# Expert blocks numbered in the order in which they fill, and scatter and store in turn on GpSimd

## The chip, the cores and the metric

The kernel runs on one core of a Trainium2 chip. Its time is the device time of one launch in microseconds; three runs of the kernel before gave 1337.54 (median), 1336.7 and 1342.43. Durations below are from one profiled execution of it, which took 1341.81 us, with a span of 1339.8 us in the trace.

## The reference

4096 tokens of width 128 (16 sequences of 256) go through four residual layers: a linear attention with an MLP, a mixture of 8 experts, a self-attention with relative positions, and the same mixture of experts again. The change is about the two expert layers:

```
logits = t @ switch_w + switch_b              # t: 4096 x 128, normalised
routes = argmax(softmax(logits));  p = max(softmax(logits))
for e in range(8):
    h = gelu(t @ w1[e] + b1[e])               # 128 -> 512
    y = h @ w2[e] + b2[e]                     # 512 -> 128
    out = where(routes == e, y, out)
x = x + out * p
```

Each token needs only the expert it is routed to.

## The kernel before, in words

Tokens lie in SBUF as `rows`, 32 tiles of 128 tokens (one token per partition), a row of 258 words each: the normalised token, the residual x, the token's number (as a count from the end) and its probability. An expert layer has two stages, each a block of engine programs; a stage begins when every engine has ended the stage before.

`route_tokens` (VectorE mostly) finds each token's expert, counts the tokens of each expert per tile, takes running sums over tiles (L249), and gives each token a slot. All slots of an expert lie together, and each expert starts at a multiple of 128, so that 40 blocks of 128 slots are enough for any route. A table `bexp` has the expert of each block (L269 to L272).

`run_experts` moves and computes. GpSimd scatters the 32 tiles with indirect DMAs into `slots_in`, an array of 40x128 rows in HBM that was cleared before (L326), and afterwards stores the 40 results (L321), each when y of its block is ready. SyncE first loads and stores the position tables of the next layer (`early`, in the first expert layer alone), waits for all 32 scatters, and then loads the 40 blocks (L340) into four buffers in turn; load k waits for y of block k-4. VectorE reads the block's expert number into a register (L418) and copies that expert's 1156 weights per partition into one of four buffers (L420), copies the transposed block out of PSUM (L426), and makes y from the second product (L432 to L435). TensorE transposes (L358) and does four products up (L366) and four down (L374); ScalarE does the gelu (L405). The order on each engine is written out by hand in `step`: block k's products up, block k+1's transpose, block k-1's products down on TensorE; expert k+2, transposed copy k+1, result k-1 on VectorE. Four blocks are unrolled, the first and last four outside a loop.

In the second expert layer the same code runs without the position tables, and the stores go to the kernel's output. Names begin with 0f or 1f for the layer, and fr and fe for the two stages.

Of the kernel before, what the change touches and what calls it, by code (L numbers as in the profile page):

```python
# [34 lines left out]
X_AT, LEFT_AT, PROB_AT = D, 2 * D, 2 * D + 1  # L35
ROW = 2 * D + 2
# [133 lines left out]

def route_tokens(nc, prefix, norm, con, L, sbias, w, WA, s_weights, prob, slot, bexp):

    with ExitStack() as stack:
# [10 lines left out]
        nblk_i = m.sb("nblocks_i", [P, E], I32)  # L184
        pre = [m.sb(f"blockprefix{i}", [P, 4 + E]) for i in range(2)]
        pos = m.sb("pos", [P, TILES, E])
        offs = m.sb("offs", [P, E])
        slotf = m.sb("slotf", [P, TILES])
        ge = m.sb("ge", [P, BLOCKS, E])
        bexpf = m.sb("bexpf", [P, BLOCKS])  # L190
# [23 lines left out]
        def _(dve):  # L214
# [26 lines left out]
            dve.memset(pre[0][:, 0:4], 0.0)  # L241
            then(dve.memset(pre[1][:, 0:4], 0.0))
# [9 lines left out]
            then(dve.tensor_scalar(nblk_i[:, :], tot[:, PAD + TILES - 1, :], float(P - 1), None, ALU.add))  # L252
            then(dve.tensor_scalar(nblk_i[:, :], nblk_i[:, :], 7, None, ALU.arith_shift_right))
            then(dve.tensor_copy(pre[0][:, 4:], nblk_i[:, :]))
            for k in range(3):
                a, b = pre[k % 2], pre[(k + 1) % 2]
                then(dve.tensor_tensor(b[:, 4:], a[:, 4:], a[:, 4 - (1 << k):4 + E - (1 << k)], ALU.add))
            bend = pre[1]

            then(dve.tensor_scalar(offs[:, :], bend[:, 3:3 + E], float(P), None, ALU.mult))  # L260
            then(dve.tensor_tensor(pos[:, :, :], tot[:, PAD:, :], cfirst[:, :, :], ALU.subtract))
            then(dve.tensor_tensor(pos[:, :, :], psr, pos[:, :, :], ALU.add))
            then(dve.tensor_tensor(pos[:, :, :], pos[:, :, :], offs[:, :].unsqueeze(1).to_broadcast(TE), ALU.add))
            then(dve.tensor_tensor(pos[:, :, :], pos[:, :, :], hot[:, :, :], ALU.mult))
            then(dve.tensor_reduce(slotf[:, :], pos[:, :, :], AX.X, ALU.add))
# [9 lines left out]
def run_experts(nc, prefix, rows, norm, con, WA, s_weights, slot, bexp, slots_in, tokens, s_cleared, again, tables=None):  # L275
# [3 lines left out]
    with ExitStack() as stack:  # L279
# [38 lines left out]
        def _(pool):  # L318
# [13 lines left out]
        def _(sp):  # L332
# [10 lines left out]
            if early:  # L343
                early.stored(sp)
# [1276 lines left out]
```

## Time and profile before

| | |
|---|---|
| median of 3 runs | 1337.54 us |
| profiled execution, its time / span | 1341.81 / 1339.8 us |
| busy share: TensorE, VectorE, ScalarE, GpSimd | 79%, 70%, 51%, 42% |
| DMA | 165.92 MB, mean 124 GB/s |
| scatters and block loop of the first expert layer | 182.8 to 328 us |
| the same of the second | 1187.9 to 1332 us |

Between the two lies the self-attention, which the change leaves alone but for a few semaphores. A time in the trace is the start of an instruction, counted from the start of the span. The busy time of a DMA instruction on GpSimd (DMA_INDIRECT) is the time in which it writes the transfer's descriptors; the data land later. "idle ... <-X" in a row is what the engine waited for last; "issue" means that it waited for nothing which the profile shows.

### The profile page before, as it was taken

What the parts mean: (1) busy time and instruction counts of PE and PEld (TensorE: products, weight loads), DVE (VectorE), ACT (ScalarE), POOL (GpSimd) and SP (SyncE); (2) the same over time, 40 slices, a digit from 0 to 9 for tenths busy, and PEclk for the clock granted to TensorE, in tenths of its full rate; (3) what the DMA queues carried; (4) which work ended last, traced back from release to release, by engine and by line L of the source; (5) the groups of instructions that cost most, each with busy time, mean ns of one, the idle gap of its engine ahead of it and who ended that gap; (6) DMA issues with size and microseconds to landing.
All of it is one profiled execution on the core that took longest, in us unless ns stands there. A gap on an engine that the chain in (4) does not pass through costs nothing. (4 is left out here: it accounts for less than half of the span.)

```text
span 1339.8 us, 31386 instructions
## 1 busy us (share of the span) xinstructions
PE 1055.2 (79%) x9281; PEld 887.9 (66%) x9281; DVE 938.7 (70%) x2968; ACT 683.0 (51%) x1705; POOL 567.5 (42%) x502
## 2 busy tenths in 40 slices
PE   3993621886444999999999999999999997801986
PEld 2892501886323788888878888888888885701886
DVE  6786641665662888888888888888888887430664
ACT  2346310444271666666666666666666664110443
POOL 2503145454000645455545545455555542045544
PEclk9997555999585999999999999999999999555999
DMA  5910053222178475665656575755656540052221
GB/s 138 231 40 1 1 209 118 73 82 77 46 300 199 114 176 137 157 156 140 161 138 168 132 177 134 162 148 145 165 137 170 128 103 1 0 193 91 79 76 52
DMA packets 75275, 165.92 MB, mean 124 GB/s; under 512 B 8250, under 2 KB 54785, under 8 KB 66529
## 3 DMA queue, kind: packets, MB, share of 16 engines
q1 hardware_dynamic: 69600, 152.75, 44.3%
q0 software_dynamic: 5632, 12.67, 2.8%
q8 instruction: 19, 0.31, 0.1%
q14 instruction: 24, 0.19, 0.0%
HBM read 130.76 MB, written 35.67 MB: 124 GB/s over the span
## 5 line engine op out<-in xcount | busy, mean ns | idle before, releaser
L1150 POOL TENSOR_SCALAR ds_scores<-ds_scores,ds_max 128x256 f32<-128x256 f32 x256 | 348.6, 1362 | 327.0 <-DVE ds_max L1369 326.8
L1361 DVE TENSOR_TENSOR ds_p2c<-ds_bank,ds_p2c 128x512 f32<-128x512 f32 x256 | 175.2, 684 | 80.2 <-PE ds_bank L1199 79.5
L1369 DVE CUSTOM_DVE_ANT_0 ds_scores<-ds_bank,ds_p2c 128x256 f32<-128x256 f32 x512 | 195.8, 419 | 0.2 <-DVE ds_p2c L1361 0.2
L1310 ACT ACTIVATE all_xt<-ds_bank 128x512 f32<-128x512 f32 x256 | 154.2, 602 | 76.3 <-PE ds_bank L1217 72.5
L1199 PE MATMUL ds_bank<-all_constants,ds_c2p_t 128*128 128x128 f32 x1024 | 159.0, 278 | 0.0
L1217 PE MATMUL ds_bank<-all_constants,ds_scores 128*128 128x128 f32 x1024 | 154.1, 272 | 1.8 <-ACT all_xt L1310 1.6
L1199 PEld LDWEIGHTS ds_bank<-all_constants,ds_c2p_t 128*128 128x128 f32 x1024 | 116.2, 141 | 35.8 <-issue 24.3
L1217 PEld LDWEIGHTS ds_bank<-all_constants,ds_scores 128*128 128x128 f32 x1024 | 119.5, 140 | 6.8 <-issue 2.2
L1190 PE MATMUL ds_bank<-ds_qr,ds_tab 64*128 64x128 f32 x1024 | 76.2, 289 | 34.2 <-DVE ds_qr L1345 30.0
L1292 ACT ACTIVATE ds_c2p_t<-ds_bank 128x256 f32<-128x256 f32 x256 | 77.8, 398 | 46.6 <-PE ds_bank L1190 46.6
L1206 PE MATMUL ds_bank<-ds_ks,ds_qs 72*128 72x256 bf16 x512 | 98.3, 273 | 1.1 <-DVE ds_max L1369 1.1
L1376 DVE TENSOR_SCALAR ds_scores<-ds_scores,ds_max 128x256 f32<-128x256 f32 x256 | 97.4, 380 | 0.0
L1190 PEld LDWEIGHTS ds_bank<-ds_qr,ds_tab 64*128 64x128 f32 x1024 | 63.9, 191 | 47.9 <-issue 39.6
L405 ACT ACTIVATE 1fe_h<-1fe_bank,1fe_expert 128x128 f32<-128x128 f32 x160 | 45.7, 369 | 96.0 <-PE 1fe_bank L366 96.0
L1292 ACT ACTIVATE ds_p2c<-ds_bank 128x256 f32<-128x256 f32 x256 | 77.6, 389 | 31.3 <-PE ds_bank L1190 31.3
L405 ACT ACTIVATE 0fe_h<-0fe_bank,0fe_expert 128x128 f32<-128x128 f32 x160 | 45.7, 369 | 87.9 <-PE 0fe_bank L366 87.9
L1345 DVE TENSOR_TENSOR ds_qr<-ds_qr,all_constants 128x2048 f32<-128x2048 f32 x32 | 73.2, 2287 | 19.7 <-DMA ds_qr<-scratch_qk 19.7
L1190 PE MATMUL ds_bank<-ds_kr,ds_tab 64*128 64x128 f32 x1024 | 74.9, 286 | 2.3 <-ACT ds_p2c L1292 1.4
L1345 DVE TENSOR_TENSOR ds_kr<-ds_kr,all_constants 128x2048 f32<-128x2048 f32 x32 | 73.2, 2287 | 4.6 <-DMA ds_kr<-scratch_qk 4.6
L321 POOL DMA_INDIRECT tokens<-0fe_y,0fe_token x40 | 50.2, 1255 | 55.2 <-DVE 0fe_y L435 47.8
L321 POOL DMA_INDIRECT out<-1fe_y,1fe_token x40 | 49.4, 1234 | 55.7 <-DVE 1fe_y L435 47.8
L1190 PEld LDWEIGHTS ds_bank<-ds_kr,ds_tab 64*128 64x128 f32 x1024 | 62.6, 188 | 13.1 <-issue 13.1
(253 smaller groups left out, 2149.0 us busy)
## 6 DMA issues: line engine op xcount, KB each, us to landing
ds_qr<-scratch_qk SPq DMA_DIRECT2D x32, 1024.0 KB, 10.7
ds_kr<-scratch_qk SPq DMA_DIRECT2D x32, 1024.0 KB, 13.7
ds_tab<-scratch_tables SPq DMA_DIRECT2D x64, 248.0 KB, 9.6
slots_in<-all_zero SPq DMA_DIRECT2D x2, 5160.0 KB, 37.7
ds_qs<-scratch_q_parts SPq DMA_DIRECT2D x32, 288.0 KB
ds_ks<-scratch_k_parts SPq DMA_DIRECT2D x32, 288.0 KB
0fe_xb<-slots_in SPq DMA_DIRECT2D x40, 129.0 KB
1fe_xb<-slots_in SPq DMA_DIRECT2D x40, 129.0 KB
```

The costliest lines, as they stand in the source:

```text
L321: pool.indirect_dma_start(tokens, bass.IndirectOffsetOnAxis(ap=token[i][:, 0:1], axis=0), y[i][:, :], None, bounds_check=TOKENS - 1, oob_i ...
L1150: pool.tensor_scalar(S[b % NS][:, 1, :], S[b % NS][:, 1, :], mx[:, 2 * b + 1:2 * b + 2], None, ALU.subtract).then_inc(s_sub1, 1)
L1190: last = pe.matmul(pb[tile][:, :].rearrange("p (r a n) -> p r a n", r=2, a=4)[:, :, a, :], TAB[half][rows, kind, c:c + P], own, start=True ...
L1199: last = pe.transpose(pt1[b % 2][:, st * SEQ + kt * P:st * SEQ + (kt + 1) * P], CT[half][:, kt, b, st * P:(st + 1) * P], con["ident"])
L1206: last = pe.matmul(pqk[b % 2][:, st * SEQ:(st + 1) * SEQ], QS[half][:, b * SEQ + st * P:b * SEQ + (st + 1) * P], KS[half][:, b * SEQ:(b + ...
L1217: last = pe.transpose(pt2[:, kt * SEQ + st * P:kt * SEQ + (st + 1) * P], S[b % NS][:, st, kt * P:(kt + 1) * P], con["ident"])
L1292: last = act.activation(dst, pb[tile][:, at * 64:(at + count) * 64].rearrange("p (g b s) -> p g b s", g=count, b=HALF), ACT.Copy)
L1310: act.activation(PT[b], pt2[:, :].rearrange("p (k s) -> p k s", k=2), ACT.Exp).then_inc(s_exp, 1)
L1345: dve.tensor_tensor(rows, rows, con["own_pos"].unsqueeze(1).to_broadcast([P, HT // 16, 16]), ALU.mult).then_inc(s_masked, 1)
L1361: dve.tensor_tensor(z, pt1[b % 2][:, :].rearrange("p (a k) -> p a k", a=2), z, ALU.add).then_inc(s_z, 1)
L1369: last = dve.tensor_tensor_reduce(out=S[b % NS][:, st, :], in0=pqk[b % 2][:, st * SEQ:(st + 1) * SEQ], in1=PC[half][:, st, b, :], scale=1. ...
L1376: dve.tensor_scalar(S[b % NS][:, 0, :], S[b % NS][:, 0, :], mx[:, 2 * b:2 * b + 1], None, ALU.subtract).then_inc(s_sub0, 1)
```

## The change

Blocks get their numbers in the order in which tiles fill them. After each tile, every expert whose count passes a multiple of 128 has filled a block, and the blocks filled by a tile are numbered by expert; blocks that stay open at the end come last. The number of blocks that can be complete after t tiles has a lower bound for any route, so block k holds only tokens of the first k+8 tiles. Four things follow in the code:

- VectorE's routing has more steps: from the running sums it makes, per tile and expert, how many blocks are full, what number the block now open will get (the next block filled, by a running minimum from behind), and from that each token's slot. The table of experts by block goes; the expert's number is a 259th word of each row, and VectorE reads it from the loaded block.
- SyncE's load of block k waits for the landing of tile k+7's scatter and of the three before, by four semaphores in turn, instead of all 32.
- GpSimd issues 12 scatters, then one scatter and one store in turn until scatter 31, then the remaining stores. A scatter waits until the one four before has landed.
- VectorE's `step` has transposed copy k+1, result k-1, expert k+2, and the last waits for the data of block k+2.

FIRST_TILES is 8; `rising` is 6, so the loads of groups 0 to 5 (blocks 0 to 23) wait tile by tile and the others for all. The parts of the routing that are left out are three prefix steps over the experts (of `open` and `fresh`), and operations of the same size as those shown. Beside it, the add-and-normalise stage uses one semaphore instead of several, and SyncE's wait for the position tables' stores at the first expert layer's end is gone.

```diff
+FIRST_TILES = E
...
             tot = cnt[1]
-            then(dve.tensor_scalar(nblk_i[:, :], tot[:, PAD + TILES - 1, :], float(P - 1), None, ALU.add))
-            then(dve.tensor_scalar(nblk_i[:, :], nblk_i[:, :], 7, None, ALU.arith_shift_right))
-            then(dve.tensor_copy(pre[0][:, 4:], nblk_i[:, :]))
...
+            then(dve.tensor_copy(full_i[:, :, :], tot[:, PAD:, :]))
+            then(dve.tensor_scalar(full_i[:, :, :], full_i[:, :, :], 7, None, ALU.arith_shift_right))
+            then(dve.tensor_copy(full[:, 1:, :], full_i[:, :, :]))
+            dve.tensor_reduce(total[:, :], full[:, :, :], AX.X, ALU.add)
+            dve.scalar_tensor_tensor(before[:, :, :], full[:, 0:TILES, :], -float(P), tot[:, PAD - 1:PAD + TILES - 1, :], ALU.mult, ALU.add)
...
+            then(dve.tensor_tensor(fresh[0][:, :, 4:], full[:, 1:, :], full[:, 0:TILES, :], ALU.subtract))
...
+            for i in range(2):
+                last = dve.tensor_tensor(number[i][:, TILES:, :], ...)
+            then(dve.tensor_tensor(number[0][:, 0:TILES, :], fresh[1][:, :, 3:3 + E], total[:, 0:TILES].unsqueeze(2).to_broadcast(TE), ALU.add))
+            then(dve.tensor_tensor(over[:, :, :], full[:, 1:, :], full[:, 0:TILES, :], ALU.subtract))
...
+            for k in range(5):
+                a, b = number[k % 2], number[(k + 1) % 2]
+                then(dve.tensor_tensor(b[:, 0:TILES, :], a[:, 0:TILES, :], a[:, 1 << k:TILES + (1 << k), :], ALU.min))
+            then(dve.tensor_tensor(place[:, :, :], psr, before[:, :, :], ALU.add))
...
-            then(dve.tensor_tensor(ge[:, :, :], con["iota_b"]..., bend[:, 4:]..., ALU.is_ge))
-            then(dve.tensor_reduce(bexpf[:, :], ge[:, :, :], AX.X, ALU.add))
-            then(dve.tensor_scalar(bexp[:, :], bexpf[:, :], float(E - 1), None, ALU.min))
...
+            def scatter(t):
+                if t >= UNROLL:
+                    pool.wait_ge(s_scat[t % UNROLL], 16 * (t // UNROLL))
+                pool.indirect_dma_start(slots_in, bass.IndirectOffsetOnAxis(ap=slot[:, t:t + 1], axis=0),
+                                        rows[:, t, :], None).then_inc(s_scat[t % UNROLL], 16)
             pool.wait_ge(s_cleared, 16)
-            for t in range(TILES):
-                pool.indirect_dma_start(...).then_inc(s_scat, 16)
+            ahead = FIRST_TILES + UNROLL
+            for t in range(ahead):
+                scatter(t)
             for k in range(BLOCKS):
+                if ahead + k < TILES:
+                    scatter(ahead + k)
                 store(k // UNROLL, k % UNROLL)
...
-            sp.wait_ge(s_scat, 16 * TILES)
...
+            def load_behind(g, i):
+                for t in range(i + FIRST_TILES - UNROLL, i + FIRST_TILES):
+                    sp.wait_ge(s_scat[t % UNROLL], 16 * (g + t // UNROLL + 1))
+                sp.sem_inc(s_go_sp, 1)
+                load(g, i)
+            rising = (TILES - FIRST_TILES) // UNROLL
...
             def expert(g, i):
-                e = dve.value_load(bexp[0:1, bass.ds(UNROLL * g + i, 1)], min_val=0, max_val=E - 1)
+                dve.wait_ge(s_x[i], 16 * (g + 1))
+                dve.sem_inc(s_go_dve, 1)
+                e = dve.value_load(xb[i][0:1, EXPERT_AT:EXPERT_AT + 1].bitcast(I32), min_val=0, max_val=E - 1)
...
-                if i < UNROLL - 2 or more:
-                    expert(g + (i + 2) // UNROLL, (i + 2) % UNROLL)
                 if i < UNROLL - 1 or more:
                     transposed(g + (i + 1) // UNROLL, (i + 1) % UNROLL)
                 if i > 0:
                     result(g, i - 1)
                 elif not isinstance(g, int) or g > 0:
                     result(g - 1, UNROLL - 1)
+                if i < UNROLL - 2 or more:
+                    expert(g + (i + 2) // UNROLL, (i + 2) % UNROLL)
```

How the instructions stand in a row shows it at three places. GpSimd in the first expert layer, before (slots_in0 is the array of slots, tokens the array of results; the number behind a name is the buffer):

```order
L326 DMA slots_in0<-all_rows,0f_slot 5120x258 [waits all_cleared0]
L326 DMA slots_in0<-all_rows,0f_slot 5120x258 x31
L321 DMA tokens<-0fe_y_0,0fe_token_0 4096x128 [waits fe_y]
L321 DMA tokens<-0fe_y_1,0fe_token_1 4096x128 [waits fe_y]
L321 DMA tokens<-0fe_y_2,0fe_token_2 4096x128 [waits fe_y]
```

and now:

```order
L353 DMA slots_in0<-all_rows,0f_slot 5120x259 [waits 0fe_scattered3]
L353 DMA slots_in0<-all_rows,0f_slot 5120x259 [waits 0fe_scattered0]
L347 DMA tokens<-0fe_y_0,0fe_token_0 4096x128 [waits fe_y]
L353 DMA slots_in0<-all_rows,0f_slot 5120x259 [waits 0fe_scattered1]
L347 DMA tokens<-0fe_y_1,0fe_token_1 4096x128 [waits fe_y]
L353 DMA slots_in0<-all_rows,0f_slot 5120x259 [waits 0fe_scattered2]
L347 DMA tokens<-0fe_y_2,0fe_token_2 4096x128 [waits fe_y]
L353 DMA slots_in0<-all_rows,0f_slot 5120x259 [waits 0fe_scattered3]
```

All 32 scatters stood ahead of the first store; now 13 do, and from there each store has a scatter behind it.

SyncE in the same layer, before (xb is the buffer of a loaded block; scratch_far_f belongs to the position tables):

```order
L941 DMA scratch_far_f<-dt_far_parts 16x8x256 x3
L340 DMA 0fe_xb_0<-slots_in0 128x258 [waits 0fe_scattered]
L340 DMA 0fe_xb_1<-slots_in0 128x258
L306 ISA
L340 ISA [waits fe_y]
L340 DMA 0fe_xb_0<-slots_in0 128x258
L315 REGISTER_ALU
L340 ISA [waits fe_y]
```

and now:

```order
L987 DMA scratch_far_f<-dt_far_parts 16x8x256 x3
L373 DMA 0fe_xb_0<-slots_in0 128x259 [waits 0fe_scattered3,0fe_scattered2,0fe_scattered0,0fe_scattered1]
L373 DMA 0fe_xb_1<-slots_in0 128x259 [waits 0fe_scattered0,0fe_scattered3,0fe_scattered1,0fe_scattered2]
L385 ISA
L341 ISA [waits 0fe_scattered3,0fe_scattered2,0fe_scattered0,0fe_scattered1]
L373 ISA [waits fe_y]
L373 DMA 0fe_xb_0<-slots_in0 128x259
L341 REGISTER_ALU [waits 0fe_scattered0]
L373 ISA [waits fe_y]
L373 DMA 0fe_xb_1<-slots_in0 128x259
```

The wait for one counter of all scatters has become four waits ahead of each load; the position tables' stores stand ahead of the first load as before.

VectorE at the first results of the first expert layer, before (expert_ is the weights' buffer, xbt the transposed block):

```order
L426 COPY 0fe_xbt_0<-0fe_bank0 128x128 [waits fe_h,fe_xt]
L432 TENSOR_TENSOR 0fe_y_0<-0fe_bank4,0fe_expert_0 128x128 [waits fe_yp]
L433 TENSOR_SCALAR 0fe_token_0<-0fe_xb_0 128x1
L435 SCALAR_TENSOR_TENSOR 0fe_y_0<-0fe_y_0,0fe_xb_0 128x128 [waits fe_yb]
L418 TENSOR_LOAD 0f_block_expert
L418 ISA x2
L420 ISA [waits fe_y]
L420 COPY 0fe_expert_0<-0f_weights 128x1156
L426 COPY 0fe_xbt_1<-0fe_bank1 128x128 [waits fe_h,fe_xt]
```

and now:

```order
L476 COPY 0fe_xbt_0<-0fe_bank0 128x128 [waits fe_h,fe_xt]
L482 TENSOR_TENSOR 0fe_y_0<-0fe_bank4,0fe_expert_0 128x128 [waits fe_yp]
L483 TENSOR_SCALAR 0fe_token_0<-0fe_xb_0 128x1
L485 SCALAR_TENSOR_TENSOR 0fe_y_0<-0fe_y_0,0fe_xb_0 128x128 [waits fe_yb]
L468 TENSOR_LOAD 0fe_xb_3 [waits fe_x3]
L468 ISA x2
L470 ISA
L470 COPY 0fe_expert_3<-0f_weights 128x1156
L476 COPY 0fe_xbt_1<-0fe_bank1 128x128 [waits fe_h,fe_xt]
```

The register load came from the table and waited for nothing, and its copy for y; it now comes from the block's own data and waits for their landing (fe_x3), one block nearer to their use.

## Rows read from the trace of the kernel before

**Rows 1.** Windows: busy us by engine (instructions), clock granted, DMA share, GB/s.
```profile
182.80:226.00 43.20, 5.26 (x9) 2.06 (x9) 8.25 (x21) 1.96 (x3) 31.87 (x32) 0.50 0.39 132
1187.90:1230.20 42.30, 0.00 (x0) 0.00 (x0) 1.52 (x2) 0.54 (x1) 31.29 (x32) 0.50 0.28 100
1230.20:1331.50 101.30, 87.62 (x680) 81.07 (x680) 62.91 (x198) 45.74 (x160) 47.51 (x39) 0.96 0.27 73
```

**Rows 2.** Instructions on slots_in: ns min/median/max, first and last start.
```profile
L340 SPq DMA_DIRECT2D 1fe_xb<-slots_in x40: 328/333/432, 1230.2 to 1324.1; - x40
L326 POOL DMA_INDIRECT slots_in<-all_rows,0f_slot x32: 956/961/1562, 182.8 to 223.2; - x32
L326 POOL DMA_INDIRECT slots_in<-all_rows,1f_slot x32: 957/961/1364, 1187.9 to 1227.7; - x32
```

**Rows 3.** Timeline: start, us, engine, line, instruction [idle before <-releaser].
```profile
182.81 1.14 POOL L326 DMA_INDIRECT slots_in<-all_rows,0f_slot  x1 [37.21 <-POOLq L173]
...
223.17 0.96 POOL L326 DMA_INDIRECT slots_in<-all_rows,0f_slot  x1 [0.30 <-issue]
226.05 17.81 SPq L340 DMA_DIRECT2D 0fe_xb<-slots_in  x8
...
228.03 0.47 PE L358 MATMUL 0fe_bank<-all_constants,0fe_xb 128*128 128x128 f32 x1 [29.12 <-DMA 0fe_xb<-slots_in]
...
236.04 0.35 DVE L435 SCALAR_TENSOR_TENSOR 0fe_y<-0fe_y,0fe_xb 128x128 f32<-128x128 f32 x1
...
327.06 0.35 DVE L435 SCALAR_TENSOR_TENSOR 0fe_y<-0fe_y,0fe_xb 128x128 f32<-128x128 f32 x1
...
1240.02 0.35 DVE L435 SCALAR_TENSOR_TENSOR 1fe_y<-1fe_y,1fe_xb 128x128 f32<-128x128 f32 x1
...
1331.14 0.35 DVE L435 SCALAR_TENSOR_TENSOR 1fe_y<-1fe_y,1fe_xb 128x128 f32<-128x128 f32 x1
```

**Rows 4.** Timeline of layer 0 at the end of the position tables.
```profile
203.50 1.53 DVE L420 COPY 0fe_expert<-0f_weights 128x1156 f32 x2 [0.32 <-issue]
203.59 1.90 SPq L941 DMA_DIRECT2D scratch_far_f<-dt_far_parts  x3
```

**Rows 5.** Line L418 in 262.2 to 263.2, then VectorE's timeline.
```profile
L418 DVEq TENSOR_LOAD <-0f_block_expert x1: 402/402/402, 262.4 to 262.4; - x1
...
261.14 0.76 DVE L420 COPY 0fe_expert<-0f_weights 128x1156 f32 x1 [0.88 <-DVE 0fe_y L435]
...
262.33 0.35 DVE L435 SCALAR_TENSOR_TENSOR 0fe_y<-0fe_y,0fe_xb 128x128 f32<-128x128 f32 x1
...
263.28 0.76 DVE L420 COPY 0fe_expert<-0f_weights 128x1156 f32 x1 [0.59 <-DVE 0fe_y L435]
```

**Rows 6.** Timeline of VectorE in layer 0's routing.
```profile
169.34 0.29 DVE L230 TENSOR_SCALAR 0fr_cand<-all_logits 128x256 f32<-128x256 f32 x1
...
174.03 2.26 DVE L249 TENSOR_TENSOR 0fr_count<-0fr_count 128x256 f32<-128x256 f32 x5
...
181.31 0.18 DVE L272 TENSOR_SCALAR 0f_block_expert<-0fr_bexpf 128x40 int32<-128x40 f32 x1
```

**Rows 7.** GpSimd's stores: their group in 240 to 320, then timeline.
```profile
L321 POOL DMA_INDIRECT tokens<-0fe_y,0fe_token x34 | 43.9, 1290 | 38.2 <-DVE 0fe_y L435 31.8 <-issue 6.4
...
261.03 0.99 POOL L321 DMA_INDIRECT tokens<-0fe_y,0fe_token  x1 [1.20 <-DVE 0fe_y L435]
263.45 1.43 POOL L321 DMA_INDIRECT tokens<-0fe_y,0fe_token  x1 [1.43 <-DVE 0fe_y L435]
...
290.05 1.03 POOL L321 DMA_INDIRECT tokens<-0fe_y,0fe_token  x1 [1.20 <-DVE 0fe_y L435]
...
328.57 0.97 POOL L321 DMA_INDIRECT tokens<-0fe_y,0fe_token  x1 [0.30 <-issue]
```

**Rows 8.** Windows around the end of the linear attention.
```profile
110.00:114.00 4.00, 1.93 (x14) 1.52 (x12) 2.54 (x9) 0.97 (x2) 0.00 (x0) 1.00 0.00 0
114.00:118.00 4.00, 0.00 (x0) 0.00 (x0) 1.43 (x7) 3.11 (x8) 0.89 (x2) 0.77 0.01 2
```

More of the change, by code:

```diff
@@ L183, in route_tokens @@
         cfirst = m.sb("counts", [P, TILES, E])
[L184 to L187, printed above, removed]
+        before = m.sb("before", [P, TILES, E])
+        full_i = m.sb("full_i", [P, TILES, E], I32)
+        full = m.sb("full", [P, 1 + TILES, E])
+        total = m.sb("total", [P, 1 + TILES])
+        fresh = [m.sb(f"fresh{i}", [P, TILES, 4 + E]) for i in range(2)]
+        open_ = [m.sb(f"open{i}", [P, 4 + E]) for i in range(2)]
+        number = [m.sb(f"number{i}", [P, TILES + PAD, E]) for i in range(2)]
+        place = m.sb("place", [P, TILES, E])
+        over = m.sb("over", [P, TILES, E])
         slotf = m.sb("slotf", [P, TILES])
-        ge = m.sb("ge", [P, BLOCKS, E])
-        bexpf = m.sb("bexpf", [P, BLOCKS])
         bank = m.banks(2)
@@ L260, in _ @@
[L260 to L265, printed above, removed]
@@ new lines, in _ @@
+            then(dve.tensor_tensor(fresh[0][:, :, 4:], full[:, 1:, :], full[:, 0:TILES, :], ALU.subtract))
+            then(dve.tensor_scalar(open_[0][:, 4:], open_[0][:, 4:], 0.0, None, ALU.is_gt))
+            for k in range(3):
+                for a, b, whole in ((open_[k % 2], open_[(k + 1) % 2], (slice(None),)), (fresh[k % 2], fresh[(k + 1) % 2], (slice(None), slice(None)))):
+                    last = dve.tensor_tensor(b[(*whole, slice(4, None))], a[(*whole, slice(4, None))],
+                                             a[(*whole, slice(4 - (1 << k), 4 + E - (1 << k)))], ALU.add)
+                then(last)
@@ new lines, in _ @@
+            none = number[0][:, TILES:TILES + 1, :].to_broadcast(TE)
+            then(dve.tensor_tensor(number[0][:, 0:TILES, :], number[0][:, 0:TILES, :], none, ALU.subtract))
+            then(dve.tensor_tensor(number[0][:, 0:TILES, :], number[0][:, 0:TILES, :], over[:, :, :], ALU.mult))
+            then(dve.tensor_tensor(number[0][:, 0:TILES, :], number[0][:, 0:TILES, :], none, ALU.add))
+            for k in range(5):
+                a, b = number[k % 2], number[(k + 1) % 2]
+                then(dve.tensor_tensor(b[:, 0:TILES, :], a[:, 0:TILES, :], a[:, 1 << k:TILES + (1 << k), :], ALU.min))
@@ new lines, in _ @@
+            then(dve.tensor_tensor(place[:, :, :], psr, before[:, :, :], ALU.add))
+            dve.tensor_scalar(over[:, :, :], place[:, :, :], float(P), None, ALU.is_ge)
+            then(dve.tensor_tensor(before[:, :, :], number[1][:, 1:1 + TILES, :], number[1][:, 0:TILES, :], ALU.subtract))
+            then(dve.scalar_tensor_tensor(over[:, :, :], before[:, :, :], 1.0, over[:, :, :], ALU.subtract, ALU.mult))
+            then(dve.tensor_tensor(over[:, :, :], over[:, :, :], number[1][:, 0:TILES, :], ALU.add))
@@ L279, in run_experts @@
+            then(dve.scalar_tensor_tensor(place[:, :, :], over[:, :, :], float(P), place[:, :, :], ALU.mult, ALU.add))
+            then(dve.tensor_tensor(place[:, :, :], place[:, :, :], hot[:, :, :], ALU.mult))
+            then(dve.tensor_reduce(slotf[:, :], place[:, :, :], AX.X, ALU.add))
+            then(dve.tensor_copy(slot[:, :], slotf[:, :]))
+def run_experts(nc, prefix, rows, norm, con, WA, s_weights, slot, slots_in, tokens, s_cleared, again, tables=None):
     with ExitStack() as stack:
@@ L701, in add_normalised @@
         shift = m.sb("shift", [P, 2 * TILES])
-        s_diff, s_sq, s_var, s_sum, s_ve, s_std, s_rstd, s_neg, s_shift, s_norm, s_gain, s_x = (m.sem(n) for n in (
-            "diff", "square", "var", "sum", "vareps", "std", "rstd", "neg", "shift", "norm", "gain", "x"))
+        s_v, s_ve, s_std, s_shift, s_norm, s_gain, s_x = (m.sem(n) for n in (
+            "v", "vareps", "std", "shift", "norm", "gain", "x"))
         GT = norm.GT
```

77 lines of the change are left out of this document (38 added, 39 removed).

## The prediction

> **What bounds the kernel now.** I read four views. First the page's span, then the windows of the two expert stages: each begins with some 43 us in which GpSimd scatters 32 tiles of rows and TensorE hardly works (5.26 us of 43.20, and 0.00 of 42.30), and only then come 101 us of block loop [rows 1]. Next the instructions on slots_in: 32 scatters at a median of 0.961 us, and in layer 1 the first load at 1230.2, behind the last scatter at 1227.7 [rows 2]. The timeline around that seam gives the latencies: the last scatter starts at 223.17 and lasts 0.96, the first load starts at 226.05 (landing and wake: 1.92), its transpose at 228.03 (1.98 from load to data), and y of block 0 (L435) ends at 236.39, in layer 1 at 1240.37 [rows 3]. So the loop waits for all scatters, by one wait on SyncE. In the loop TensorE is busy 87.62 us for 40 blocks, 2.19 each [rows 1], and y comes about every 2.4 us, so TensorE and the round of VectorE around it set the pace. GpSimd is used 47.51 us of 101.3 there [rows 1]: it follows.
>
> **The change, part by part.** Three terms: the loop starts earlier, the routing before it gets longer, and in the first half of the loop GpSimd has two DMAs to issue per block.
>
> *Earlier start.* A load of block k now waits for tiles up to k+7. Counted from the first scatter, which starts at 182.81 and 1187.9 [rows 2, 3]: the eighth starts 9.04 later (the first pitch is 1.14 and 0.30, six are 0.96 and 0.30 and a little), ends 0.96 later and is seen 1.92 later: 11.9. In layer 1 this is the start of the first load, where before it was 42.3. In layer 0 SyncE first has the position tables to store: its last three issues start at 203.59 and take 1.90 [rows 4], so the load starts at 205.6, which is 22.8 instead of 43.2. The expert number is now read from the loaded block, so VectorE's first two weight copies, which stood finished in the wait before (203.50, layer 0 [rows 4]), fall behind the landing: two copies of 0.76 and, ahead of the first, a register load. From its start to its copy's I estimate 0.7: it lasts 0.40 itself, and the one at 262.4 had its copy at 263.28, 0.9 later, with a wait for y in between [rows 5]. I take 1.7 us in layer 0 (all four loads leave at once) and 2.2 in layer 1 (the second load is 1.27 behind the first). With y of block 0 10.3 and 10.2 us after the load before [rows 3], it now comes at 22.8+10.3+1.7 = 34.8 and 11.9+10.2+2.2 = 24.3, against 53.6 and 52.5 before.
>
> *Longer routing.* Behind the running sums (L249), VectorE ran to the end of L272: 176.3 to 181.5, 5.2 us [rows 6]. In its place stand about 27 operations on 256 elements and some small ones. From L249, five of them in 2.26, one with its wait costs 0.46; a copy or scalar operation 0.33 (0.29 of L230 and the wait); a scalar_tensor_tensor, by 0.35 for 128 elements [rows 3] and 0.13 more, 0.53. Three casts and shifts 1.1; sum, base, open and fresh 1.6; three prefix steps of a small and a large one 1.7; fill, number, over and three combinations 2.8; five minima 2.3; place to slot 3.8: 13.3. That is **8.1 us more in each layer**, on the path, since GpSimd starts behind the stage's end. The five more short fills lie in VectorE's wait for the counts' matmul; uncovered they cost about 0.5 by their sizes.
>
> *GpSimd in the loop.* Scatters 12 to 31 now alternate with stores 0 to 18, and tile k+7, the last that load k needs, stands behind store k-6 and the y it waits for. GpSimd's pair costs at least 0.96+0.30 and 0.97+0.30 (the store at 328.57 came with its y long ready: idle 0.30 [rows 7]), 2.53. The stores of the loop take 1.29 on average, not 0.97 [rows 7]. The rows show when: at 261.03 the store started ahead of VectorE's copy (261.14) and took 0.99; at 263.45 the copy (263.28) had started first, and it took 1.43 [rows 5, 7]. A store starting under the copy waits for its end. So the pair lies between 2.53 and 2×1.59 = 3.18 (both at the loop's mean). Where the copies fall follows from the chain: scatter 0.96, landing 1.92, load 1.98, register load 0.7, copy start: 5.6 us behind the scatter's start, 0.4 to 0.5 into a pair's period of 2.6, and over at its 1.2, when the store starts. It grazes it. I take **2.70**; each 0.1 us on it costs 19 intervals in two layers, 3.8 us.
> The Trainium skill (SBUF — State Buffer, "Who interferes with whom") says that VectorE in a two-port mode and GpSimd take the shared ports for a whole instruction, and the later one is fully blocked; it speaks against putting more GpSimd DMAs beside these copies. The durations above agree, and VectorE's copies, 0.76 in the rows here, are not the ones that lose. By the rule alone, with each start just behind a copy's, a pair would cost up to 2.53+2×0.76 = 4.05; by the rows it is 3.18 at their mean.
>
> *The chain through the loop.* y of block j needs load j+2, whose scatter j+9 stands ahead of store j-3. From that store's start S: scatter -1.3, landing 2.9, load 1.98, register load and copy start 0.7, then copy to end of y 1.54 (261.14 to 262.68 [rows 5]): S+5.9. GpSimd wants it with 0.8 to spare for its wake at 3 periods, 8.1: it is there, by 1.4 us, so GpSimd's issue is the pace and not the chain. Then: store 0 at y0+0.8, store 19 at 19×2.70 = 51.3 later, y of block 22 5.9 later, since its load needs the last scatter. That is y0+58.0, where before it came y0+52.9 (store 22 started at 290.05, y 0.8 earlier [rows 7]): 5.1 us lost.
>
> *The second half.* 17 more blocks took 38.1 us (289.3 to 327.4 [rows 3, 7]). The register load now waits for the data of its block, issued 0.2 behind y of four blocks earlier and 1.98 under way: 2.2 us behind y of k-2, where before it started 0.3 ahead of the end of y of k-1, at about 2.1 (262.4 against 262.68 [rows 5]). It is later by 0.1 on average, and VectorE goes in order. Between 0 (the TensorE round hides it) and 0.4 per block (the longest shift, behind a short interval of 2.1), I take 0.1: 1.7 us.
>
> *Per layer, first scatter to last y.* Layer 1: before 143.6 (1187.9 to 1331.5 [rows 2, 3]); now 24.3+58.0+38.1+1.7 = 122.1, and with the routing 130.2: 13.4 less. Layer 0: before 144.6; now 34.8+58.0+39.8 = 132.6, with the routing 140.7: 3.9 less. The rest: rows of 259 instead of 258 words, fewer semaphores in the add-and-normalise stage, one wait less at layer 0's end: 0, nothing there waits on them, at most 0.5 either way. Sum: **17 us less**. On the profiled execution's 1341.8 that is 1324.5; on the runs' median of 1337.5, 1320.5, which I forecast as 1321.
>
> **Rivals.**
> *Both DMAs of a pair meet the copies.* For it: three of four stores do now, one of each kind stands in [rows 7]. Against: they do because y starts both the store and the copy, and this coupling goes. At 3.18 the sum is 17 - 38×0.48 = -1: no change, 1339.
> *The pair costs 3.46 (slower).* Place: scatters 12 to 31 and stores 0 to 18 on GpSimd. Each waits as long as the longest measured store, 1.43+0.30. 38×0.76 = 29 us more than my 17: 12 slower, 1349. It decides from a pair of 3.15 us on, where the gain is gone. Against: a copy lasts 0.76 in 3.46 us and can hardly meet two starts fully.
> *TensorE falls to half its clock in the mixed half.* Its share would be 2.19/2.70, 81%, in gaps under 1 us. The granted clock stood at 1.00 (2.4 GHz) with TensorE busy 1.93 of 4 us, and fell to 0.77 only in a stretch of none [rows 8]. A block at 1.2 GHz takes about 4.4 us; over 22 blocks in two layers that is 2×22×1.7 = 75 more: 1395. The Trainium skill (TensorE: Matmul & The Clock Gate, "A second HAM failure mode: psum-queue depth-cycling") tells of short idles between groups of matmuls that make the gate oscillate; the window above does not show it.
> *The data's landing paces the second half.* At 0.4 per block, 34×0.3 = 10 more: 7 us less than before, 1331. For it: the margin is 0.1 us. Against: TensorE's own 2.19 leaves 0.2 per block.
> *The early start is worth nothing*, because the pace of scatters decides anyway: the scatters' pitch of 1.265 is half a block's, so no.
>
> **How the numbers follow.** A run set can tell about 0.5%, 6.7 us, from no change. Forecast (gain 10 to 24, 1314 to 1328): 0.52. Better than that (pair 2.53, no loss in the second half: 17+6.5+3.4 = 27, 1310.5): 0.06. Landing paces: 0.12, half of it still over 6.7. Pair near 3.18: 0.15. Pair at 3.3 or more: 0.12. Clock: 0.03. Faster: 0.52+0.06+0.06 = 0.64. Same: 0.06+0.15, less a part that ends slower, 0.20. Slower 0.16. Range: 1310 to 1341, which leaves out the slow rivals and little below.
>
> **What would show it.** VectorE between the end of L249's counterpart and the stage's end: 13.3 us, not 5.2. First load 11.9 us behind the first scatter in layer 1, 22.8 in layer 0. GpSimd without idle beyond 0.3 between store 1 and scatter 31, pitch of stores 2.70, then 2.4 with idle. DMA durations on GpSimd: scatters in the loop near 1.0, stores near 1.1. Granted clock 1.00 from y0 on. The forecast is wrong if stores in the first half are over 3.1 us apart, if GpSimd idles there for y, or if the second half runs at over 2.6.

## The result

Over 20 runs each, before took 1341.59 us and the changed kernel 1335.56 us (median): ratio 0.995, 95% interval 0.993 to 0.9971. It is faster by 6 to 7 us, where 17 were forecast. A later set of 6 runs gave 1329.52 against 1341.26, ratio 0.9928 (0.9901 to 0.9955). The profiled execution spans 1334.2 us, before 1339.8.

The windows of the profile after: start and end, length, then busy us by engine, the granted clock, DMA share and GB/s. For each layer the three are first scatter to y of block 0, y0 to y of block 22, and from there to the last y.

```profile
187.70:223.00 35.30, 12.14 (x45) 8.30 (x46) 10.67 (x28) 4.27 (x11) 12.66 (x13) 0.52 0.34 106
223.00:283.90 60.90, 48.86 (x374) 43.57 (x373) 35.37 (x110) 25.16 (x88) 44.91 (x41) 1.00 0.38 113
283.90:323.10 39.20, 34.36 (x275) 31.56 (x273) 25.30 (x81) 19.57 (x65) 21.02 (x17) 1.00 0.24 67
1198.00:1223.50 25.50, 6.55 (x36) 5.92 (x37) 3.75 (x9) 2.88 (x9) 12.61 (x13) 0.54 0.29 89
1223.50:1286.50 63.00, 48.78 (x372) 43.52 (x371) 35.43 (x110) 25.15 (x88) 46.05 (x41) 1.00 0.38 110
1286.50:1325.90 39.40, 34.63 (x277) 31.79 (x275) 25.43 (x81) 18.29 (x64) 20.02 (x17) 1.00 0.23 64
```

From the first scatter to the first y it was 52.5 us in layer 1 and is now 25.4; but the middle stretch, 52.5 before, is now 63.0 us with GpSimd busy 46 of them. In the middle TensorE has 2.4 GHz (1.00) throughout.

The timeline after answers to [rows 3] and [rows 2] (start, us, engine, line, instruction): first scatter, first load and last operation of y of block 0, 22 and 39.

```profile
1198.03 1.06 POOL L353 DMA_INDIRECT slots_in<-all_rows,1f_slot  x1 [76.07 <-POOLq L176]
...
1210.14 0.34 SPq L373 DMA_DIRECT2D 1fe_xb<-slots_in  x1
...
1223.11 0.35 DVE L485 SCALAR_TENSOR_TENSOR 1fe_y<-1fe_y,1fe_xb 128x128 f32<-128x128 f32 x1
...
1286.14 0.35 DVE L485 SCALAR_TENSOR_TENSOR 1fe_y<-1fe_y,1fe_xb 128x128 f32<-128x128 f32 x1
...
1325.56 0.35 DVE L485 SCALAR_TENSOR_TENSOR 1fe_y<-1fe_y,1fe_xb 128x128 f32<-128x128 f32 x1
```

Read so for both layers of two profiled executions, in us (the second is the changed kernel run again in the experiments):

| stretch | before, layers 0 / 1 | forecast | after | after, again |
|---|---|---|---|---|
| routing's first step to first scatter | 14.8 / 14.8 | +8.1 | 22.3 / 22.2 | 22.3 / 22.2 |
| first scatter to y0 | 53.6 / 52.5 | 34.8 / 24.3 | 35.2 / 25.4 | 35.1 / 24.5 |
| y0 to y22 | 52.9 / 52.5 | 58.0 | 60.9 / 63.0 | 61.8 / 61.9 |
| y22 to last y | 38.1 / 38.6 | 39.8 | 39.2 / 39.4 | 40.5 / 39.8 |
| first scatter to last y | 144.6 / 143.6 | 132.6 / 122.1 | 135.3 / 127.9 | 137.4 / 126.2 |

With 7.4 us more routing per layer the two stages are worth 10.2 and 9.7 us, not 17. The rest of the program is touched only by the side edits and the wider rows, but is not constant: from the position terms of attention to the second routing it took 759.8 us in the profile of before, 766.1 and 763.8 in the two of after, and between 760.7 and 765.9 in ten other kernels that have the same attention. The two profiles with the old expert layers have 759.8 and 761.7, the eleven with the new ones 763.2 on average, so a small cost of the change there, of 2 us or so, is not excluded. It is this stretch above all, with smaller shifts ahead of the first routing, that makes the spans differ by 5.6 and 11.1 us around stages that differ by 10.

**How GpSimd spends the middle.** Groups of GpSimd in the first profile after, us 1223 to 1280 (count, busy us, mean ns, idle us before and what ended it); they answer to the group in [rows 7]:

```profile
L347 POOL DMA_INDIRECT out<-1fe_y,1fe_token x20 | 24.5, 1226 | 17.1 <-DVE 1fe_y L485 12.2 <-issue 4.9
L353 POOL DMA_INDIRECT slots_in<-all_rows,1f_slot x19 | 19.6, 1030 | 5.8 <-issue 5.5 <-DVE 1fe_y L485 0.3
```

Ten of the 12.2 us lie ahead of the first store. A pair is one store and one scatter; its price is the distance from one store's start to the next one's. Stores 0, 5 and 19 of layer 1:

```profile
1224.28 1.29 POOL L347 DMA_INDIRECT out<-1fe_y,1fe_token  x1 [9.97 <-DVE 1fe_y L485]
...
1238.44 1.32 POOL L347 DMA_INDIRECT out<-1fe_y,1fe_token  x1 [0.30 <-issue]
...
1279.79 1.52 POOL L347 DMA_INDIRECT out<-1fe_y,1fe_token  x1 [0.78 <-DVE 1fe_y L485]
```

From store 0 to store 19 a pair takes 2.80 us in layer 0 and 2.92 in layer 1 (2.83 and 2.86 in the second profile), not 2.70. The timeline of a few pairs, GpSimd first, then VectorE's copies beside them:

```profile
1244.10 0.99 POOL L347 DMA_INDIRECT out<-1fe_y,1fe_token  x1 [0.30 <-issue]
1245.39 1.11 POOL L353 DMA_INDIRECT slots_in<-all_rows,1f_slot  x1 [0.30 <-issue]
1247.25 1.32 POOL L347 DMA_INDIRECT out<-1fe_y,1fe_token  x1 [0.75 <-DVE 1fe_y L485]
1248.88 0.96 POOL L353 DMA_INDIRECT slots_in<-all_rows,1f_slot  x1 [0.30 <-issue]
1250.14 1.50 POOL L347 DMA_INDIRECT out<-1fe_y,1fe_token  x1 [0.30 <-issue]
...
1244.80 0.87 DVE L470 COPY 1fe_expert<-1f_weights 128x1156 f32 x1 [1.52 <-DMA 1fe_xb<-slots_in]
...
1246.95 0.76 DVE L470 COPY 1fe_expert<-1f_weights 128x1156 f32 x1 [0.50 <-DVE 1fe_y L485]
...
1250.02 0.76 DVE L470 COPY 1fe_expert<-1f_weights 128x1156 f32 x1 [1.04 <-DMA 1fe_xb<-slots_in]
```

The stores at 1247.25 and 1250.14 began 0.30 and 0.12 into a copy and ended 0.86 us after its end; the scatter at 1245.39, which began near a copy's end, took 0.15 longer than 0.96. The copy at 1244.80 began under a running store and lasted 0.87. And the store at 1247.25, store 8, had waited 0.75 for its y, which the forecast said would not happen. This is rare: of the 38 DMAs of the pairs three waited so in layer 1 and one in layer 0, 1.5 and 0.6 us beyond the usual 0.30 in all. The way of the data back from store 8: y8 needs load 10, whose last tile is scatter 17.

```profile
1237.17 0.96 POOL L353 DMA_INDIRECT slots_in<-all_rows,1f_slot  x1 [0.30 <-issue]
...
1241.50 0.33 SPq L373 DMA_DIRECT2D 1fe_xb<-slots_in  x1
...
1246.10 0.35 DVE L485 SCALAR_TENSOR_TENSOR 1fe_y<-1fe_y,1fe_xb 128x128 f32<-128x128 f32 x1
```

Scatter to load 4.33, load to copy (1244.80) 3.30, copy to the end of y 1.65, wake 0.80: 10.08 us. GpSimd issues seven DMAs on this way, 8.86 us at 1.265 each.

### The profile page after: what moved, and what is told of

The parts are those of the page before. It is cut to its first block and busy times, and to the rows that moved or that the text cites. A ratio compares the mean times of both kernels' runs of the same rounds, so it can differ in the third digit from the quotient of the medians.

```text
span 1334.2 us, 31677 instructions
## 1 busy us (share of the span) xinstructions
PE 1062.7 (80%) x9281; PEld 889.5 (67%) x9281; DVE 953.9 (71%) x3013; ACT 683.2 (51%) x1705; POOL 563.3 (42%) x502
## 5 line engine op out<-in xcount | busy, mean ns | idle before, releaser
L1245 PEld LDWEIGHTS ds_bank<-all_constants,ds_c2p_t 128*128 128x128 f32 x1024 | 116.2, 140 | 35.8 <-issue 24.3
L1391 DVE TENSOR_TENSOR ds_qr<-ds_qr,all_constants 128x2048 f32<-128x2048 f32 x32 | 73.2, 2288 | 22.3 <-DMA ds_qr<-scratch_qk 22.3
L470 DVE COPY 1fe_expert<-1f_weights 128x1156 f32 x40 | 31.2, 781 | 55.0 <-DMA 1fe_xb<-slots_in 35.2
L1226 PE MATMUL ds_bank<-ds_qr,ds_tab 128*128 128x128 f32 x512 | 67.3, 286 | 3.4 <-ACT ds_c2p_t L1338 1.9
```

The source lines that it names most:

```text
L1245: last = pe.transpose(pt1[b % 2][:, st * SEQ + kt * P:st * SEQ + (kt + 1) * P], CT[half][:, kt, b, st * P:(st + 1) * P], con["ident"])
L1391: dve.tensor_tensor(rows, rows, con["own_pos"].unsqueeze(1).to_broadcast([P, HT // 16, 16]), ALU.mult).then_inc(s_masked, 1)
```

## The experiments

**Side edits alone,** on the kernel before (the semaphores of the add-and-normalise stage and of V's memset, and the wait `early.stored`; the row keeps its 258 words):
```
-            if early:
-                early.stored(sp)
...
-        s_diff, s_sq, s_var, s_sum, s_ve, s_std, s_rstd, s_neg, s_shift, s_norm, s_gain, s_x = ...
+        s_v, s_ve, s_std, s_shift, s_norm, s_gain, s_x = ...
...
-            dve.memset(V[:, :, :, DB:], 1.0).then_inc(s_one, 1)
+            dve.memset(V[:, :, :, DB:], 1.0)
```


> The kernel before with the side edits alone: one semaphore in the add-and-normalise stage, no wait for the position tables' stores, no semaphore on the memset of V. Theory A (the profiled execution after lost 6.3 us in the attention and won 2.5 before the first routing by chance, the side edits cost nothing): 0 us against before within 2; in its profile the first routing starts at 168.0 or up to 2.5 us earlier, first ds_qr to the second routing 757 to 767. Theory B (the side edits or the shifted buffers cost some 4 us outside the expert stages): 3 to 5 us slower than before, and the attention stretch at 765 or more.

Measured: 1342.15 us against 1341.48, ratio 1.001 (0.9992 to 1.0028). They cost nothing, as forecast. No run has the row of 259 words alone.

**The copy as a reduction over one element**, in the changed kernel:
```
-  dve.tensor_copy(WB[i][:, :], WA[:, bass.ds(e, 1), :]...)
+  dve.tensor_reduce(WB[i][:, :].unsqueeze(2), WA[:, bass.ds(e, 1), :]..., AX.X, ALU.max)
```


> The changed kernel, with the weight copy on VectorE written as a tensor_reduce over one element: same values, about 1.35 us instead of 0.76, but of another kind of operation. Theory A (the pair of a scatter and a store costs 2.80 and 2.92 us instead of 2.53 since GpSimd's DMAs wait at their start for a copy that holds what they need): all DMA_INDIRECT of the block loop at 0.96 to 1.05, pair pitch 2.53 to 2.6 in both layers though VectorE has 0.6 us more per block; y0 to y22 falls by 3 to 6 us a layer, but the second half rises from 39.3 to 43 or more. Theory B (the pitch is set by the late y, and the copies' durations only show beside it): pair pitch 2.9 to 3.2, with GpSimd idle for y.

Measured: 1342.94 us, ratio 1.0009 (0.9992 to 1.0026). The groups of its profile, us 1240 to 1290:

```profile
L470 DVE TENSOR_REDUCE 1fe_expert<-1f_weights 128x1156 f32 x18 | 24.4, 1357 | 13.0 <-DVE 1fe_y L485 10.5 <-DMA 1fe_xb<-slots_in 2.5
L347 POOL DMA_INDIRECT out<-1fe_y,1fe_token x18 | 17.8, 987 | 13.4 <-issue 7.5 <-DVE 1fe_y L485 5.9
L353 POOL DMA_INDIRECT slots_in<-all_rows,1f_slot x15 | 14.5, 966 | 4.6 <-issue 4.6
```

Every DMA is at its short time: it is the copy that stretches them. Yet the pair stayed at 2.83 and 2.84, and each of the first 20 stores waited for its y: from the copy's start to the end of y it is now 2.14 us, 0.5 longer. A way of the data 0.5 us longer was thus enough to make it the pace, the first sign that its slack was well under the 1.4 us of the prediction.

**More scatters ahead of the first store:**
```
-            ahead = FIRST_TILES + UNROLL
+            ahead = 28 if tables else 20
```


> The changed kernel with 28 scatters ahead of the first store in layer 0 and 20 in layer 1, instead of 12: GpSimd stood idle for 19.7 and 10.0 us there. Theory A (GpSimd's issue is the pace of the first half): 16 pairs less in layer 0 at 2.80 become blocks at 2.41, 6 us less, and 8 pairs less in layer 1 at 2.92, 4 us less: y0 to y22 at 55 and 59, the total 8 to 10 us below the changed kernel, 14 to 17 below before. Theory B (the chain scatter, landing, load, y is the pace): 0 to 2 us less.

Measured: 1318.14 us, ratio 0.9814 (0.9794 to 0.9834): 23 us under before and 17 under the changed kernel of the first set, 11 under the second. y0 to y22 is 56.8 and 55.5 us, where theory A had 55 and 59. First scatter to last y, over both layers, is 251.6 us, 11.6 less than in the changed kernel's first profile where 10 were expected; the rest of the 17 lies outside these stages (attention 761.8 us for 766.1). In layer 1 the last scatter starts 31.9 us behind y0 instead of 54.2, and no load waits for a scatter in the middle stretch any more.

**Routing and numbering alone:** `ahead = TILES`, and all loads wait for all scatters, as before.

> The changed kernel with all 32 scatters ahead of the first store and the loads waiting for all of them: new numbers, new routing and the expert number from the block, no overlap. Theory A (the longer routing is paid in full): first scatter 7.4 us later behind the start of the routing in each layer, y0 2 us later behind the last scatter (the first two weight copies behind the landing), 17 blocks of the second half 39.3 instead of 38.1, so 2.7 us on 39 blocks: 24 us slower than before in all, 1.8%. Theory B (something hides part of the routing): under 15 us slower.

Measured: 1363.66 us, ratio 1.0164 (1.0144 to 1.0184), 22 us slower. The routing's 14.8 us are paid in full (first scatter 7.4 us later in each layer). From there to the last y it takes 3.0 and 3.1 us more than before, in the first block and in the loop together.

**The changed kernel again.**

> The changed kernel once more, for a second profiled execution. Theory A (the price of the pair is fixed by the instruction order): stores 0 to 19 again 2.80 us apart in layer 0 and 2.92 in layer 1, within 0.03, and from the first scatter to the last y 135 and 128 us; the 6.3 us by which attention was longer in the first profile do not come back (760 to 763.5 us from the first position row to the second routing), and the median is 1335 to 1336. Rival B (the loop settles into one of several phases, and the phase changes from execution to execution): the pitch differs from the first profile by more than 0.05 us in at least one layer. Rival C (the change makes attention longer): attention 766 us again.

Measured: 1329.52 us, ratio 0.9928 (0.9901 to 0.9955), 6 us below the expected median; the stretches are in the last column of the table above. The pitch, that is the price of the pair, moved by 0.04 in layer 0 and 0.07 in layer 1, in part beyond the 0.05 of rival B, but the sum of the two middle stretches did not: 123.9 and 123.7 us. Attention was 763.8, neither as short as theory A had it nor 766 again. So the loop's shortfall repeats; of the 5.5 us between the two profiled spans attention has 2.3, and what makes the rest of the difference between the two sets is not shown.

**Short copies,** in the changed kernel (buffers filled once, 4 columns copied; left out: the right weights):
```
-  dve.tensor_copy(WB[i][:, :], WA[:, bass.ds(e, 1), :]...)
+  dve.tensor_copy(WB[i][:, 0:4], WA[:, bass.ds(e, 1), 0:4]...)
...
+  for i in range(UNROLL):
+      dve.tensor_copy(WB[i][:, :], WA[:, i, :]).then_inc(s_pre, 1)
+  dve.wait_ge(s_pre, UNROLL)
```


> The changed kernel, with the four weight buffers filled once per layer with experts 0 to 3 and only 4 of the 1156 columns copied in the loop, so that most tokens meet the wrong expert's weights (left out: the right weights). VectorE's copy falls from 0.76 us to under 0.1 and no long copy can meet a DMA of GpSimd. Theory A (the stores that the copy stretches, and the y that come late behind it, make the pair dearer than 2.70): every scatter and store 0.96 to 1.00 us, the pair 2.53 to 2.60, y0 to y22 54 to 57 us in both layers (61 and 63 in the changed kernel), last stretch 36 to 39: 1317 to 1324 us. Rival B (the pitch comes from the landings or from GpSimd's own issue, not from VectorE): pair 2.75 or more, time within 4 us of the changed kernel (1332 to 1339).

Measured: 1317.51 us, ratio 0.9819 (0.9796 to 0.9842). Its groups, us 1212 to 1269:

```profile
L347 POOL DMA_INDIRECT out<-1fe_y,1fe_token x22 | 21.8, 989 | 19.2 <-DVE 1fe_y L485 13.2 <-issue 6.0
L353 POOL DMA_INDIRECT slots_in<-all_rows,1f_slot x19 | 18.4, 966 | 5.8 <-issue 4.6 <-DVE 1fe_y L485 1.2
L470 DVE COPY 1fe_expert<-1f_weights 128x4 f32 x22 | 4.4, 198 | 26.6 <-DMA 1fe_xb<-slots_in 14.9 <-issue 6.1 <-DVE 1fe_y L485 5.6
```

The time is what theory A said, the pair is not: 2.73 and 2.63, with no DMA stretched; y0 to y22 is 59.4 and 57.1. VectorE waits 14.9 us for loads. Of the 38 DMAs of the pairs five waited for y in layer 0 and three in layer 1, 3.3 and 1.4 us in all: with the stretching gone it is the way of the data that keeps the pair above its bare price.

**All 32 scatters ahead,** loads still by their tiles: `ahead = TILES`.

> The changed kernel with all 32 scatters ahead of the first store (no alternation), the loads still waiting only for the tiles that they need. Theory A (GpSimd stands idle between its 12th scatter and the first y, and a scatter there is free): scatters end 40.3 us after the first. In layer 0 y0 comes at 35 and no store is late: y0 to y22 52 to 55 us. In layer 1 y0 comes at 25, the four buffers of y are full at 33 and the first store only starts at 40.3, so y4 comes at 43 to 44 and y0 to y22 is 59 to 62. Together 10 to 12 us less than the changed kernel: 1320 to 1326, some us above the kernel with 28 and 20 scatters ahead. Rival B (it is the alternation that brings the gain, stores must begin with the first y): 1334 or more.

Measured: 1326.62 us, ratio 0.9897 (0.9877 to 0.9918). y0 to y22 is 55.8 us in layer 0 and 65.3 in layer 1, where y4 waits 9.56 us for store 0:

```profile
1234.23 0.29 DVE L482 TENSOR_TENSOR 1fe_y<-1fe_bank,1fe_expert 128x128 f32<-128x128 f32 x1 [9.56 <-DMA out<-1fe_y,1fe_token]
```

The alternation of scatters and stores is thus worth nothing in layer 0, where this does better than the change; the gain is the early load. In layer 1 it is worth 2 to 3 us (63.0 and 61.9 with it); there I had the wait but made the stretch some 4 us too short.

**All ahead with short copies** (left out: the right weights).

> The kernel with all scatters ahead of the first store, and the weight copies shortened to 4 columns as in the other kernel (left out: the right weights). Theory A (past the scatters the pace is VectorE's, with the copy of 0.76 us in each step): y0 to y22 falls by 3 to 10 us in layer 0 and the last stretch from 39 to 33 to 37. Rival B (the pace there is that of the chain through TensorE and the activations, or of the landings): y0 to y22 and the last stretch within 1.5 us of the kernel without the short copies.

Measured: 1314.49 us, ratio 0.9816 (0.9772 to 0.986). y0 to y22 falls by 3.5 and 3.2 us, the last stretch by 2.3 in both layers: 0.14 per block, though the copy fell by 0.56. VectorE's copy is a part of the pace there, not all of it. In layer 0 this is just inside theory A's ranges (3 to 10, and a last stretch of 36.9 for 33 to 37), but far from the 0.56 per block that a pace of VectorE's alone would give.

**Two scatters more ahead:**
```
-            ahead = FIRST_TILES + UNROLL
+            ahead = FIRST_TILES + UNROLL + 2
```


> The changed kernel with 14 instead of 12 scatters ahead of the first store, so 18 pairs instead of 20, and two pairs more between a scatter and the store that waits for what hangs on it. In the changed kernel the way from the start of scatter k+7 to the start of store k-2 took a median of 10.1 us in layer 1 (landing and load's issue 3.7, load to copy 3.2, copy to end of y 1.65, the wake 0.8, and what was waited on GpSimd); GpSimd's seven DMAs on it take 8.9 at 1.265 each. Theory A (this way had no slack, so each stretched DMA is lost for good): with 11 DMAs on it, 13.9 us, the stores never wait for y, the pair costs 2.63 to 2.72 us in both layers (2.83 to 2.92 before), y0 to y22 57.5 to 59.5 us. Together 5 to 8 us less than the changed kernel: 1322 to 1328. Rival B (the stretched DMAs alone set the pitch): pair still 2.80 or more, y0 to y22 60.5 to 61.5, 1328 to 1334.

Measured: 1320.65 us, ratio 0.984 (0.981 to 0.987): below theory A's range. Waits of SyncE's queue between y0 and y22 in layer 1 (us, times, longest), in the changed kernel:

```profile
SPq L378 <- DMA slots_in<-all_rows,1f_slot: 28.6, 14, 3.1
SPq L373 <- DVE 1fe_y L485: 14.0, 9, 7.7
```

and in this one:

```profile
SPq L373 <- DVE 1fe_y L485: 36.7, 22, 8.5
SPq L378 <- DMA slots_in<-all_rows,1f_slot: 5.9, 5, 1.6
```

The loads wait for free buffers, no longer for scatters. But the pair still costs 2.80 and 2.85 with GpSimd at 0.30 idle between its DMAs:

```profile
L347 POOL DMA_INDIRECT out<-1fe_y,1fe_token x22 | 24.6, 1118 | 13.8 <-DVE 1fe_y L485 9.5 <-issue 4.3
L353 POOL DMA_INDIRECT slots_in<-all_rows,1f_slot x17 | 19.3, 1135 | 5.2 <-issue 4.3 <-DVE 1fe_y L485 0.9
```

So rival B had the pair and theory A the time. What brings the time is the place of the last scatter: it came 48.1 us after y0 instead of 53.8, two pairs earlier, and y22 followed it by 8.1 and 8.2 us (layer 1, against the second profile of the changed kernel). In layer 0 it came 6.4 us earlier and y22 only 3.7, so there it set the end in part. The stores fell behind here (in layer 1 they began a median of 3.7 us after their y), and this cost nothing: with four buffers of y VectorE never waited for a store, as it did with all scatters ahead.

**The same with short copies** (left out: the right weights).

> The same 14 scatters ahead, with the weight copies shortened to 4 of 1156 columns (left out: the right weights). Theory A (without stretched DMAs and with slack on the way, GpSimd goes at the pace of its own issue): pair 2.53 to 2.57 us in both layers, where the kernel with short copies and 12 scatters ahead had 2.73 and 2.63, and no idle over 0.31 us between two DMAs of the pairs; y0 to y22 54.5 to 57 us, 1308 to 1315 us. Rival B (something else than that way holds the stores back): pair 2.62 or more, y0 to y22 57 to 59.5, 1315 to 1319.

Measured: 1309.26 us, ratio 0.9749 (0.9714 to 0.9784); the pair is 2.56 us in both layers, y0 to y22 53.4 and 52.9, over 1 us shorter than expected, the time inside the range. Its groups, us 1214 to 1255:

```profile
L353 POOL DMA_INDIRECT slots_in<-all_rows,1f_slot x17 | 16.4, 965 | 5.2 <-issue 4.9 <-DVE 1fe_y L485 0.3
L347 POOL DMA_INDIRECT out<-1fe_y,1fe_token x16 | 15.8, 989 | 4.9 <-issue 2.7 <-DVE 1fe_y L485 2.1
```

The pair is as theory A had it, and none of its DMAs waited for y. The pair's price, in us, layers 0 / 1 (from store 0 to store 19, with 14 ahead to store 17):

| | copies whole | copies short |
|---|---|---|
| 12 ahead | 2.80 / 2.92, again 2.83 / 2.86 | 2.73 / 2.63 |
| 14 ahead | 2.80 / 2.85 | 2.56 / 2.56 |

Only with both gone is it GpSimd's bare issue of 2.56. The way of the data alone (short copies, 12 ahead) holds it 0.17 and 0.07 above, the stretching alone (whole copies, 14 ahead) 0.24 and 0.29, nearly as much as both together (0.24 to 0.36).

**Loads ahead of the tables' stores,** 24 and 20 scatters ahead:
```
-            ahead = FIRST_TILES + UNROLL
+            ahead = 24 if tables else 20
...
             if early:
                 early.loads(sp)
-                early.stores(sp)
...
             for i in range(UNROLL):
                 load_behind(0, i)
+            if early:
+                early.stores(sp)
```


> A version meant to beat both: 24 scatters ahead of the first store in layer 0 and 20 in layer 1, and in layer 0 the first four loads stand ahead of the stores of the position tables on SyncE's queue. Theory A: the first load leaves 12 us behind the first scatter instead of 23 in layer 0, and VectorE is then free 20.5 us behind it and no longer waits 6 us for the load: y0 29.5 to 30.5 us behind the first scatter (35.4 before), y0 to y22 56 to 58. Against the kernel with 28 and 20 scatters ahead 4 to 6 us less: 1312 to 1315. Rival B (the stores of the tables, or TensorE's part in them, push the first blocks back anyway, or the earlier loads slow the tables): y0 33 us or more, 1317 to 1320.

Measured: 1313.9 us, ratio 0.9804 (0.9771 to 0.9837). SyncE's queue and VectorE in layer 0:

```profile
199.69 5.74 SPq L372 DMA_DIRECT2D 0fe_xb<-slots_in  x4
205.47 0.43 SPq L984 DMA_DIRECT2D scratch_tables<-dt_tables  x1
...
207.52 0.69 DVE L1038 TENSOR_TENSOR dt_far_parts<-dt_far_rest,dt_far_parts 128x512 bf16<-128x512 f32 x1
208.65 0.77 DVE L471 COPY 0fe_expert<-0f_weights 128x1156 f32 x1 [0.44 <-issue]
```

The first load leaves 11.8 us behind the first scatter (187.9), the tables' store is not later, and y0 comes at 29.2 instead of 35.4. This has the lowest median of the versions that compute everything: 28 us under before, and 16 to 22 under the change. Its interval overlaps that of the kernel with 28 and 20 scatters ahead, but first scatter to last y over both layers is 246.6 us against 251.6 there.

## Why the prediction was right in sign and wrong in size

- **Early start: right.** The first load left 12.1 us behind the first scatter in layer 1 (11.9) and 23.1 in layer 0 (22.8); y0 was 0.4 and 1.1 us later than said, and 0.3 and 0.2 in the second profile.
- **Longer routing: right, 0.7 us too dear.** 7.4 us per layer, not 8.1: a scalar_tensor_tensor of 256 elements took 0.42, where I had scaled 0.53 from the one on 128; with three of them this is 0.3 of the 0.7. The experiment with the numbering alone shows that it is paid in full.
- **"It grazes it. I take 2.70": the step that failed, the term mis-sized.** The pair cost 2.80 and 2.92, which with 19 intervals is 1.8 and 4.2 us, 6 of the 7.9 that the loop lost beyond the forecast. Of 38 DMAs from store 0 on in layer 1, scatters averaged 1.03 and stores 1.21, against 0.97 and 0.99 without long copies; of the 0.36 us above the 2.56 of the last table 0.28 are that and 0.08 waits for y. In layer 0 it is 0.21 and 0.03 of 0.24. I had put 0.17 for the stretching, nothing for waits, and 2.53 for the bare pair. The copy did not keep its place in the period: it follows the load's landing in some rounds and y in others ([1.52 <-DMA], [0.50 <-DVE] above), so it meets either DMA. I had put one phase on it, inside bounds of 2.53 to 3.18 whose middle was nearer. With two scatters more ahead, where hardly a store of the pairs waits, the pair still costs 2.80 and 2.85: the stretching alone exceeds what I put.
- **"It is there, by 1.4 us": wrong too, at a smaller price.** I put 5.9 us from a store's start to the y three blocks on (the terms add up to 5.8); in the instance above (store 5 at 1238.44, y8 at 1246.45) it was 8.0. In layer 1 the medians over blocks 3 to 22 are 3.8 us from scatter to load (I had 2.88), 3.3 from load to copy (2.68) and 1.65 from copy to y (1.54): 8.7 for 7.1. I took landing and load from [rows 3], where the queues carried nothing else; in the loop scatters, loads and stores share them (that this is the reason is not shown). With the wake of 0.8 this makes 9.5 us, more than the 8.86 of seven bare DMAs and less than the 9.8 to 10.2 that seven of them took at the measured price of the pair. So y is mostly just in time, and only the four waits counted above, 2.1 us in both layers, are its price in the pair. By itself this way holds the pair at 2.73 and 2.63, as the short copies show. GpSimd idling for y was one of the prediction's signs of being wrong.
- **y22 behind the last pair:** 5.9 said, 6.7 to 7.1 measured from store 19, by the same lengths: 1 us per layer.
- **Second half: right.** 39.2 and 39.4 us for 39.8 (40.5 and 39.8 in the second profile); the side edits: nothing, as said.
- **Rivals.** The clock stood at 1.00; the landing did not pace the second half; both DMAs do meet copies, but at 2.8 to 2.9 rather than 3.18; the copies lose now and then as well, which I had ruled out.

The loop's terms make 7.9 us (2.9 and 5.0), the routing and the rest give 0.9 back: 17.3 becomes 10.3, and 10.2 was measured. The difference to the 5.6 us of the spans lies mostly in attention, and is within its spread of 6 us; what makes that spread stays open. The medians of the two sets, 6 and 12 us below before, lie on either side of the 10 of the stages. Open is also where in the queues the 0.9 us between scatter and load arises.

## What to carry to other kernels

When one engine's queue both feeds a loop and drains it, work out the way from a feeding transfer round to the drain that depends on it, with durations taken where the queues are full, and put the last feeding transfer early: its place set the end here, while drains may lag as long as buffers are free. Fill the feeding engine's idle time before the first drain first; two scatters more ahead were worth about as much as the whole change. Where a long instruction of one engine stretches those of another, price it over all phases in which they can meet, not at the one that a steady state seems to give.

## What the hardware showed that I had not expected

- An indirect DMA of GpSimd that starts under VectorE's 1156-column copy ends about 0.85 us after the copy's end, nearly its whole length of 0.96 (median 0.84 in layer 0 and 0.85 in layer 1 of the first profile after, over 50 such DMAs; two rows above have 0.86). The five exceptions began within 0.05 us of the copy's start and were not stretched. Under copies of 4 columns or the reduction the groups above have means of 0.965 to 0.989.
- The reverse is rarer: of 32 copies that started under such a DMA in the first profile after, 27 took 0.76 to 0.79 us and five took 0.87 to 1.05; in the second profile 10 of 44 took over 0.79.
- A tensor_reduce over one element moves the same 1156 columns without the stall, but takes 1.36 us.
